# Retention and a mixture of experts on one core: the mask by head moves from the queries to the keys

## What is computed

```python
attn = jnp.einsum('bhid,bhjd->bhij', qc, kc) * D
o_intra = jnp.einsum('bhij,bhje->bhie', attn, vc)
o_inter = jnp.einsum('bhid,bhde->bhie', qc * decay_q[None, :, :, None], S)
S_new = decay_s[None, :, None, None] * S + jnp.einsum('bhjd,bhje->bhde', kc * decay_k[None, :, :, None], vc)
return (S_new, o_intra + o_inter)
```

## Time and profile before

| | us |
|---|---|
| median of 3 runs | 280.47 (279.89 to 281.02) |
| the profiled execution | 278.63 |
| its span from first to last instruction | 276.6 |
| TensorE busy | 266.6 (96%), 3614 records and as many weight loads |
| VectorE busy | 202.5 (73%) |
| ScalarE busy | 184.9 (67%) |
| GpSimd busy | 211.0 (76%) |
| granted TensorE clock | 0.999 of full speed |

### The profile page before, as it was taken

The page is one execution under the profiler, slowest core; times in us unless marked ns, Lnnn a source line. Parts: engine busy times, 40 slices in busy tenths (PEclk is TensorE's granted clock), DMA queues, the critical chain, the costliest instruction groups (busy, mean ns, idle before and its releaser), DMA issues.

```text
span 276.6 us, 8905 instructions
## 1 busy us (share of the span) xinstructions
PE 266.6 (96%) x3614; PEld 209.6 (76%) x3614; DVE 202.5 (73%) x489; ACT 184.9 (67%) x306; POOL 211.0 (76%) x221
## 2 busy tenths in 40 slices
PE   7978998989999999999999999999999999999995
PEld 5655776767887788778887788778887788788883
DVE  2779368976949985695748876595857679898783
ACT  2475548739885488675794588675794577777771
POOL 2235887989999988987989878987989848744552
PEclk9999999999999999999999999999999999999999
DMA  6429246005150152223250251123420251153102
GB/s 205 137 73 279 71 172 197 15 6 188 43 154 5 78 192 63 91 76 115 84 154 4 80 189 42 40 68 79 130 76 2 81 179 41 54 154 116 73 0 76
DMA packets 13576, 26.85 MB, mean 97 GB/s; under 512 B 1120, under 2 KB 6496, under 8 KB 13536
## 3 DMA queue, kind: packets, MB, share of 16 engines
q1 hardware_dynamic: 13536, 26.30, 29.7%
HBM read 24.07 MB, written 2.23 MB: 95 GB/s over the span
## 4 chain that ended last, share of the span: by engine, by line
PE 67%; POOL 10%; issue 10%; DVE 5%; DMA 4%; ACT 2%; POOLq 1%; DVEq 0%
POOL act_lo L1130 9%; PE h_ps L344 8%; PE y_ps L365 7%; PE h_ps L346 7%; PE y_ps L359 7%; PE h_ps L345 7%; PE y_ps L360 7%; PE bank L498 4%; PE bank L432 2%; PE bank L510 2%; DMA scale<-w 2%; PE bank L462 2%; PE bank L520 2%; PE bank L483 1%; DMA scale<-scratch 1%
## 5 line engine op out<-in xcount | busy, mean ns | idle before, releaser
L1130 POOL TENSOR_TENSOR act_lo<-act_f,act_hi 128x512 fp32r<-128x512 f32 x112 | 144.1, 1312 | 38.3 <-ACT act_f L972 37.7
L762 DVE SCALAR_TENSOR_TENSOR act_s<-h_ps,scale 128x1024 f32<-128x1024 f32 x64 | 77.7, 1215 | 25.4 <-issue 12.8
L967 ACT ACTIVATE act_hi<-act_s 128x1024 fp32r<-128x1024 f32 x64 | 68.6, 1072 | 23.1 <-DVE act_s L762 22.9
L972 ACT ACTIVATE act_f<-act_s 128x1024 f32<-128x1024 f32 x64 | 67.9, 1061 | 1.0 <-POOL act_lo L1130 1.0
L344 PE MATMUL h_ps<-x_hi,w_lo 128*128 128x512 f32 x128 | 53.6, 418 | 0.8 <-DVE act_s L762 0.8
L359 PE MATMUL y_ps<-act_hi,w_lo 128*128 128x512 f32 x128 | 52.4, 410 | 0.0
L346 PE MATMUL h_ps<-x_hi,w_hi 128*128 128x512 f32 x128 | 50.7, 396 | 0.0
L360 PE MATMUL y_ps<-act_hi,w_hi 128*128 128x512 f32 x128 | 50.5, 395 | 0.0
L345 PE MATMUL h_ps<-x_lo,w_hi 128*128 128x512 f32 x128 | 50.4, 394 | 0.0
L365 PE MATMUL y_ps<-act_lo,w_hi 128*128 128x512 f32 x128 | 40.4, 397 | 1.1 <-POOL act_lo L1130 1.0
L344 PEld LDWEIGHTS h_ps<-x_hi,w_lo 128*128 128x128 f32 x128 | 24.1, 188 | 7.6 <-DVE act_s L762 1.5
(11 more groups left out here) (123 smaller groups left out, 384.9 us busy)
## 6 DMA issues: line engine op xcount, KB each, us to landing
scale<-scratch SPq DMA_DIRECT2D x32, 512.0 KB, 4.2
x_t_in<-x_tr SPq DMA_DIRECT2D x8, 256.0 KB, 5.0
x_all<-x SPq DMA_DIRECT2D x8, 256.0 KB, 4.9
out<-out_sb SPq DMA_DIRECT2D x8, 256.0 KB, 4.2
scale<-w SPq DMA_DIRECT2D x1, 768.0 KB, 5.0
cst<-constants SPq DMA_DIRECT2D x1, 417.0 KB, 5.4
cst<-constants SPq DMA_DIRECT2D x1, 296.0 KB, 5.6
cst<-constants SPq DMA_DIRECT2D x1, 260.0 KB, 2.7
```

The source lines that it names most:

```text
L762: nc.vector.scalar_tensor_tensor(out=act_s[:, u % 2], in0=h_ps[:, u % 2], scalar=0.0, in1=scale[:, f % 2, e].unsqueeze(1).to_broadcast([P, ...
L967: nc.scalar.activation(act_hi[:, u % 4], act_s[:, u % 2], ACT.Square).then_inc(act_hi_ready, 1)
L972: nc.scalar.activation(act_f[:, u % 2], act_s[:, u % 2], ACT.Square).then_inc(act_f_ready, 1)
L1130: nc.gpsimd.tensor_tensor(act_lo[:, u % 4, n], act_f[:, u % 2, n], act_hi[:, u % 4, n].bitcast(F32), ALU.subtract).then_inc(pool_low_ready, 1)
```

## The change

The mask by head moves to the keys. mask_k on ACT writes two copies of k_t into k_m, ordered so that for each chunk the 64 keys of the even heads and the 64 of the odd heads stand side by side. scores multiplies, for each chunk and pair, these 128 columns (32 rows, stationary) with the chunk's 64 queries, q_d, which carry gamma ** (i + 1); the table then holds gamma ** -(j + 1) where j is not beyond i, and has half the columns. Both heads of a pair now lie on the partitions of a score bank.

outputs_within sums over 128 rows, which are both heads, with the two heads' v beside zeros as stationary: 32 products in place of 64, all in slot 15. v_z gets a fifth slot, and v must stand on other partitions than it comes on: copy_v writes it by halves (8 instructions in place of 4, the logits in 2 in place of 4), and a new step, shift_v, copies two half-height blocks across the partition halves, with a semaphore of its own for which outputs_within waits.

Steps move with it. On ACT mask_k stands after copy_k, and in the settled loop after square(u + 1); decay_q waits for the projection alone and in f = 0 stands before scale_h(2). Ahead of the loop project_v(1) stands before project_k(1), outputs_within(0) between them, center_piece(1) before outputs_before(0); outputs_within(1) is one step. The load of W1 behind av_done comes as two DMAs with two semaphores.

```diff
-        q_m = sb("q_m", [P, 2, 2, TILE])
+        k_m = sb("k_m", [P, 2, CHUNKS, 2, CHUNK])
-        v_z = sb("v_z", [P, 2, GROUPS * PAIRS, 4, DH])
-        attn = sb("attn", [P, 2, PAIRS, GROUPS, 2, CHUNK])
+        v_z = sb("v_z", [P, 2, GROUPS * PAIRS, SLOTS, DH])
+        attn = sb("attn", [P, 2, PAIRS, CHUNKS, CHUNK])
...
-            sp.dma_start(w1_in[:, 2:], w1[2:].rearrange("e d h -> d e h")).then_inc(w1_loaded, DMA)
+            sp.dma_start(w1_in[:, 2:4], w1[2:4].rearrange("e d h -> d e h")).then_inc(w1_loaded, DMA)
+            sp.dma_start(w1_in[:, 4:], w1[4:].rearrange("e d h -> d e h")).then_inc(w1_rest_loaded, DMA)
...
             def scores(s):
                 b = s % 2
-                pe.wait_ge(q_m_ready, s + 1)
+                pe.wait_ge(k_m_ready, s + 1)
+                pe.wait_ge(q_d_ready, s + 1)
...
-                for g in range(GROUPS):
-                    for c in range(2):
-                        for pair in range(PAIRS):
-                            rows = slice(PW * pair, PW * (pair + 1))
-                            last = pe.matmul(score_bank(s, pair)[CHUNK * c:CHUNK * (c + 1), P * g:P * (g + 1)],
-                                             chunk_of(k_t[rows, b], 2 * g + c), chunk_of(q_m[rows, b], 2 * g + c),
-                                             start=(g == 0), stop=(g == GROUPS - 1), skip_group_check=True)
+                for n in range(CHUNKS):
+                    for pair in range(PAIRS):
+                        rows = slice(PW * pair, PW * (pair + 1))
+                        last = pe.matmul(chunk_of(score_bank(s, pair), n),
+                                         k_m[rows, b, n].rearrange("p j i -> p (j i)"),
+                                         chunk_of(q_d[rows, b], n), start=(n == 0), stop=(n == CHUNKS - 1),
+                                         skip_group_check=True)
...
-            def outputs_within(s, groups):
+            def outputs_within(s):
                 b = s % 2
-                if groups[0] == 0:
-                    pe.wait_ge(attn_ready, PAIRS * (s + 1))
-                    pe.wait_ge(update_ready, 2 * (s + 1))
-                for g in groups:
-                    for j in range(2):
+                pe.wait_ge(attn_ready, PAIRS * (s + 1))
+                pe.wait_ge(update_ready, 2 * (s + 1))
+                pe.wait_ge(v_shifted, s + 1)
+                for g in range(GROUPS):
+                    for c in range(2):
                         for pair in range(PAIRS):
-                            for c in range(2):
-                                rows = slice(CHUNK * c, CHUNK * (c + 1))
-                                pe.matmul(chunk_bank(s, c)[out_rows(pair, c), CHUNK * g:CHUNK * (g + 1)],
-                                          v_z[rows, b, PAIRS * g + pair, 2 * j:2 * j + 2], attn[rows, b, pair, g, j],
-                                          start=(g == 0 and j == 0), stop=False, skip_group_check=True)
+                            pe.matmul(chunk_bank(s, c)[out_rows(pair, c), CHUNK * g:CHUNK * (g + 1)],
+                                      v_z[:, b, PAIRS * g + pair, 3 * c:3 * c + 2], attn[:, b, pair, 2 * g + c],
+                                      start=(g == 0), stop=False, skip_group_check=True)
...
-                    if n == 13:
-                        outputs_within(a, (0, 1))
                     if n == 15:
-                        outputs_within(a, (2, 3))
+                        outputs_within(a)
                         outputs_before(a)
...
             project_q(1)
+            project_v(1)
+            outputs_within(0)
             project_k(1)
-            outputs_within(0, (0, 1, 2, 3))
-            project_v(1)
+            center_piece(1)
             outputs_before(0)
-            center_piece(1)
...
             def decay_q(s):
-                dve.wait_ge(q_m_ready, s + 1)
+                dve.wait_ge(q_done, s + 1)
...
+            def mask_k(s):
+                if s == 0:
+                    act.wait_ge(k_t_first, 1)
+                else:
+                    act.wait_ge(k_t_ready, s)
                 if s >= 2:
                     act.wait_ge(qk_done, earlier(s))
...
+                keys = k_t[:, s % 2].rearrange("p (n i) -> p n i", i=CHUNK)
+                nc.scalar.activation(k_m[:, s % 2, :, 0], keys, ACT.Copy, scale=cst[:, C_EVEN:C_EVEN + 1])
+                nc.scalar.activation(k_m[:, s % 2, :, 1], keys, ACT.Copy, scale=cst[:, C_ODD:C_ODD + 1]
+                                     ).then_inc(k_m_ready, 1)
...
                 for g in range(GROUPS):
-                    nc.scalar.copy(x_all[:, s % X_RING, g, P:WIDE], v_place(s, g)[:, P:WIDE])
-                    last = nc.scalar.activation(v_z[:, s % 2, PAIRS * g:PAIRS * (g + 1), ::3],
-                                                v_place(s, g)[:, 0:P].rearrange("p (n h d) -> p n h d", h=2, d=DH),
-                                                ACT.Copy, scale=precision[:, s % STAT_RING, g:g + 1])
+                    for c in range(2):
+                        last = nc.scalar.activation(
+                            v_z[side[c], b, PAIRS * g:PAIRS * (g + 1), 2 * c:2 * c + 3:2],
+                            v_place(s, g)[side[c], 0:P].rearrange("p (n h d) -> p n h d", h=2, d=DH),
+                            ACT.Copy, scale=precision[side[c], s % STAT_RING, g:g + 1])
                 last.then_inc(v_z_ready, 1)
+
+            def shift_v(s):
+
+                act.wait_ge(v_z_ready, s + 1)
+                nc.scalar.copy(v_z[0:P // 2, s % 2, :, 3], v_z[P // 2:, s % 2, :, 2])
+                nc.scalar.copy(v_z[P // 2:, s % 2, :, 1], v_z[0:P // 2, s % 2, :, 2]).then_inc(v_shifted, 1)
...
             copy_v(0)
+            shift_v(0)
             copy_route()
             high_qk()
+            copy_v(1)
             copy_k(1)
-            mask_q(1)
-            copy_v(1)
             high_x_t(2)
             copy_o(0)
+            mask_k(1)
             high_piece(1)
+            shift_v(1)
...
                 square(u + 3)
+                if a < TILES:
+                    shift_v(a)
                 square(u + 4)
```

More of the change, by code:

```diff
@@ L28 @@
 WIDE = P + EXPERTS
+SLOTS = 5
 HALVES = HIDDEN // P
@@ L53 @@
 C_DECAY = C_DK + P
-C_SECOND = C_DECAY + HEADS * CHUNK
+C_SECOND = C_DECAY + PAIRS * CHUNK
 C_WO = C_SECOND
@@ L152, in k_bank, with v_bank @@
             return h_bank[1] if s == 1 else bank0[:]
+        def v_bank(s):
+            return (bank1[:], h_bank[2])[s] if s < 2 else bank2[:]
         def v_place(s, g):
@@ L590, in _ @@
             w1_product(0, 0)
-            outputs_within(1, (0, 1))
+            outputs_within(1)
             project_k(2)
@@ L594, in _ @@
             w1_product(0, 1)
-            outputs_within(1, (2, 3))
             outputs_before(1)
@@ L673, in decay_scores @@
                 for pair in pairs:
-                    table = cst[:, C_DECAY + P * pair:C_DECAY + P * (pair + 1)]
+                    table = cst[:, C_DECAY + CHUNK * pair:C_DECAY + CHUNK * (pair + 1)]
                     nc.vector.tensor_tensor(
-                        attn[:, s % 2, pair].rearrange("p g j i -> p g (j i)"),
-                        score_bank(s, pair).rearrange("p (g n) -> p g n", n=P),
-                        table.unsqueeze(1).to_broadcast([P, GROUPS, P]), ALU.mult).then_inc(attn_ready, 1)
+                        attn[:, s % 2, pair], score_bank(s, pair).rearrange("p (n i) -> p n i", i=CHUNK),
+                        table.unsqueeze(1).to_broadcast([P, CHUNKS, CHUNK]), ALU.mult).then_inc(attn_ready, 1)
             def mask_updates(s):
@@ L818, in _ @@
                     scale_h(f, 1)
+                    decay_q(a)
                     scale_h(f, 2)
-                    decay_q(a)
                     statistics(p, 1)
@@ L923, in copy_v @@
                     act.wait_ge(rank_step, RANK_STEPS * (s - X_RING + 1))
+                b, side = s % 2, (slice(0, P // 2), slice(P // 2, P))
+                nc.scalar.copy(x_all[:, s % X_RING, 0:GROUPS - 1, P:WIDE],
+                               v_bank(s)[:, 0:WIDE * (GROUPS - 1)].rearrange("p (g w) -> p g w", w=WIDE)[:, :, P:])
+                nc.scalar.copy(x_all[:, s % X_RING, GROUPS - 1, P:WIDE], v_place(s, GROUPS - 1)[:, P:])
                 for g in range(GROUPS):
[L925 to L928 removed]
+                    for c in range(2):
[3 more added lines that the diff above has]
+                            ACT.Copy, scale=precision[side[c], s % STAT_RING, g:g + 1])
                 last.then_inc(v_z_ready, 1)
+            def shift_v(s):
+                act.wait_ge(v_z_ready, s + 1)
+                nc.scalar.copy(v_z[0:P // 2, s % 2, :, 3], v_z[P // 2:, s % 2, :, 2])
+                nc.scalar.copy(v_z[P // 2:, s % 2, :, 1], v_z[0:P // 2, s % 2, :, 2]).then_inc(v_shifted, 1)
             def copy_o(s):
@@ L983, in _ @@
             act.wait_ge(first_loaded, DMA)
-            mask_q(0)
+            mask_k(0)
             copy_v(0)
+            shift_v(0)
```

(17 more changed lines are left out.)

17 lines of the change are left out of this document (6 added, 11 removed).

## The result

The changed kernel takes **286.08 us** (median of 6, 283.89 to 287.91) where the kernel before took 280.18 (6 runs, 278.23 to 281.04): 1.025 times as long, with a 95% interval of 1.021 to 1.030. By the medians that is +5.9 us, by the ratio some 7. The forecast was 281.4, its range 277.2 to 283.2. Some executions of a kernel hold stretches in which TensorE's clock is halved, and the ratios leave out the disturbed ones. The profiled execution took 287.91 us with a span of 286.0 and a mean granted clock of 0.976. It is the longest of the six, so about 1.8 us of what its rows show is missing in the median.

What follows compares the result with a forecast made beforehand. TensorE was taken to bound the kernel from 66 us, with ACT and POOL on the path before. Settled tiles -0.7, f = 0 +1.05 and head +0.6 gave +0.9, so 281.4 us by the median; range 277.2 to 283.2.

Steps and rivals of the forecast that it cites:

- The scores: Score products in each tile: weight loads set the pace, 1.87 us for 1.14, +0.73 a tile.
- Rival 1: Score loads hide behind other quarters' products; scores stay at 1.14 us, each settled tile saves 0.88; 277.6 us, chance 0.25.
- The outputs within: Products within chunks: the slot at n = 13 goes, -0.98 a tile; slot 15 runs four abreast, +0.10.
- Rival 2: Products within chunks, 128 rows, run only two abreast: +0.9 in each of five settled tiles; 287 us, chance 0.10.
- The rule of the Trainium skill: Loads overlap products only in other row groups: 5.2 us for the 64 records, about 310 us; 1 in 50.
- -0.98: Time a settled tile gains when the slot of products within chunks at n = 13 goes, 0.87 + 0.11 us.
- the term of -0.7 for the settled tiles: Tiles 3 to 7, where TensorE is the bound, together get 0.7 us shorter.
- copy_v: ACT's copies of logits and values go from 1.3 to 2.3 us with eight half-height copies, +0.95.
- f = 0: Tile f = 0: the longer copies pass through square(2) and POOL's act_lo to TensorE's wait; with slot 15, +1.05 us.
- The head: Ahead of f = 0: later v_z, partly given back by halved products and an ended stall, +0.6 us (-0.5 to +1.7).
- The stall of 1.13 us: Unexplained TensorE stall in outputs_before(0) in the head, expected to end with 128 fewer records and loads ahead of it.
- -0.15 a tile: Change of a settled tile: 0.73 for the scores, -0.98 and +0.10 for the outputs within.

Runs made afterwards that it cites:

- e7: Kernel before with all products within chunks in slot 14, those with the state still in slot 15: 279.41 us for 278.69 (1.002).
- e10: Changed kernel with two 512-column products of zeros ahead of the scores of tile 2 in f = 0, none in the head: 285.53 us (1.026).
- e3: Kernel before with only the value copies cut into eight half-height ones, sides taking turns: 283.97 us for 279.01 (1.019).
- e6: Changed kernel with 512-column products of zeros in TensorE's waits, one in the head and two in f = 0: 285.82 us (1.024).
- e5: Changed kernel with full-height value copies into a plain buffer and four copies from there into the zero-filled one: 279.89 us for 278.69 (1.004).

## Why the prediction was wrong

**The scores: right.** Tile 7 of the changed kernel:

```profile
216.86 0.33 PE L467 MATMUL bank<-q_d,k_m 32*128 32x64 f32 x3
...
217.02 0.28 PE L467 MATMUL bank<-q_d,k_m 32*128 32x64 f32 x3
...
217.13 0.28 PE L467 MATMUL bank<-q_d,k_m 32*128 32x64 f32 x3
...
218.81 0.50 PE L365 MATMUL y_ps<-act_hi,w_lo 128*128 128x512 f32 x1
```

```profile
L467 PEld LDWEIGHTS bank<-q_d,k_m x288: 181/187/333, 54.2 to 218.5; 32*128 32x128 f32 x144
```

Loads of 187 ns and a step of 0.11 are what the prediction named. 216.86 to 218.81 is 1.95 us for 1.14, +0.81 where +0.73 stood. Rival 1 is out. In f = 0, where the clock was halved, the same step was 0.21 to 0.22 (54.58, 54.80, 55.01).

**The outputs within: right in the mechanism, too low by 0.14 a tile.** 229.71 to 230.74 is 1.03 us:

```profile
229.71 1.10 PE L502 MATMUL bank<-attn,v_z 128*32 128x64 f32 x64
230.74 0.94 PE L514 MATMUL bank<-q_d,state 32*32 32x64 f32 x64
```

Rival 2 decided from 1.1 on and had 1.76, so it is out; that its 287 lies near the measured time is chance. The rule of the Trainium skill ("TensorE: Matmul & The Clock Gate", Part 3) that the prediction weighed needed 5.2, and the trace differs. Products of 128 rows do run abreast, since 64 of them one by one, at the prediction's 0.055, would take 3.5 us. Against the 0.79 of the earlier trace rows that is +0.24, not +0.10. With these two sizes the sum is 0.81 - 0.98 + 0.24 = +0.07 a tile, and 31.68 against 31.60 measured +0.08. So the term of -0.7 for the settled tiles had the wrong sign and was 1.1 us too low. What e7 adds: the -0.98 is earned by the halved products, none of it by the slot that is saved.

**copy_v: the first step that failed.** "8 half-height ones, which cost what their columns cost, 0.12 + 8 x 0.27" took the step of full-height copies from the earlier trace rows. Measured: 3.12 us, +1.8 for +0.95. No bounds were given for it, though an ACT operation of half height stood nowhere among the rows. The trace of before has the nearer row: ACT's copy of the outputs, whose partitions change each time, and the squares behind it, whose partitions do not.

```profile
127.60 0.37 ACT L936 COPY o_t<-bank 128x256 f32<-128x256 f32 x1 [3.27 <-PE bank L510]
127.99 0.37 ACT L937 COPY o_t<-bank 64x256 f32<-64x256 f32 x1
128.37 0.37 ACT L938 COPY o_t<-bank 64x256 f32<-64x256 f32 x1
128.76 1.06 ACT L967 ACTIVATE act_hi<-act_s 128x1024 fp32r<-128x1024 f32 x1
129.72 1.04 ACT L972 ACTIVATE act_f<-act_s 128x1024 f32<-128x1024 f32 x1
```

Steps of 0.38 and 0.39 for copies of 0.37, against 0.96 for squares of 1.06. With 0.376 a step the term would have been +1.8, in f = 0 and in the head.

**f = 0: right in its path, too small by the copies.** That copy_v(2) goes through square(2) and POOL's act_lo to TensorE's wait was right: e10 shows the wait at 66.50, where e3 has 1.1 us of it. e3, which has the half copies and nothing else, lost 2.3 us in f = 0, not 1.05; e6 and e10, the changed kernel at full clock, lost the same 2.3. What the prediction did not see is that scores(2) itself waits for v_z: on paper it lay "before that wait" and was free, in the profile it is the 2.0 us at 54.23.

**The head: one half right, one wrong.** The stall of 1.13 us in outputs_before(0) is gone as forecast; its 64 products run without a gap, from 22.69 to 23.55 in the changed kernel. Without its 0.95 for the copies the head's term is -0.35; with full-height copies it measured +1.1 from the first copy of k on (e5, which shifts 0.8 longer), so the masks, the order and the scores there were up to 1.5 off together; which of them, no run separates. With the half-height ones route_outputs starts at 14.02 instead of 11.25, +2.8 where "v_z comes 1.9 us later" stood, the difference being again the 0.9 of the copies. And copy_v stands in the head twice, while the prediction priced it once: copy_v(1) takes 3.1 us as well (19.27 to 22.38), and copy_k(1) and copy_o(0) come behind it on ACT. TensorE waits 1.4 us for copy_o(0) in e3, where the kernel before has no such wait. At f = 0 that makes +2.8 in e3 and +3.2 in e6, for the +0.6 forecast.

**The clock: not foreseen.** No term and no rival had it, since the earlier trace rows show 0.99 to 1.00. Here it cost 0.9 us in the head and 1.5 in f = 0 of the profiled execution, of which a kernel that keeps it has lost 0.6 again by f = 2. It goes with the scatter of the six executions (mean clock 0.976 to 0.988: 287.0 to 287.9 us; 0.991 to 0.994: 283.9 to 285.2), and does not account for the rest: e3, at full clock in three of its four executions, lost 5.0 us.

**The sum.** With +1.8 in place of +0.95, in f = 0 and once in the head, and +0.07 in place of -0.15 a tile, the same sum gives 0.35 + 1.9 + 1.45 = +3.7, or 284.2. Of the 1.9 that are missing, the head has most: e6 measured +3.2 there at full clock, where this sum has 1.45, and +2.3 in f = 0, where it has 1.9. The clock's share comes on top in the executions in which it fell. How much of each is in the median is not settled.

## What to carry to other kernels

Before an instruction is cut into smaller ones, look in the trace for neighbours of the new form, not of the old: starts, not durations, show whether two of them overlap, and on ACT copies that take turns between partition halves do not. ACT had 8 us to spare in a settled tile and was still the path in the first three tiles; cost such a change there first, once for each time that the step stands there, and ask of each wait which other engines stand behind the late one. And compare starts from an event that both kernels share: 1.0 us of what looked like the clock's price was there before the fill. The gaps by "issue" here kept to a place in the instruction list: adding a few instructions moved one, packing small ones closer brought four, and six long products between two runs of short ones took them away.

## What the runs showed of the hardware

ACT: copies of 64 partitions and 128 columns, 0.36 us long, start 0.255 us apart on one side and 0.37 apart where the side changes. TensorE: 64 records with 128 rows and 32 stationary columns take 1.03 us, 0.016 each; 181 records and as many loads in 2.2 us end in a gap of 1.8 us by "issue" with a packet of instructions begun shortly ahead of it; a packet holds about 258 of TensorE's instructions (7228 in 28, 6204 in 24). The clock: TensorE idled for 2.0 us ahead of the scores of tile 2 in both e3 and the changed kernel; behind it the clock stayed at 1.00 in the one and fell to 0.66 over ten microseconds in the other. What else decides it stays open.
